# Moving VectorE's squares and state additions one step later, and finding scatter rows one group sooner, in a two-layer kernel

## What is computed

```
x = x + gated_slot_attention(norm(x))   # 16 heads, DK 64, DV 128, 64 slots; two recurrences over time
x = x + fp8_linear(norm(x))
x = x + windowed_attention(norm(x))     # 16 heads of 128, rope, window 64
x = x + routed_experts(norm(x))         # 64 experts, top 4, plus 2 shared experts
```

```
hk = hk * g_t + k_t x p_t ;  ok = q_t . hk          # state S of the kernel
pv = softmax(ok)
hv = hv * g_t + p_t x v_t ;  o = pv . hv            # state R of the kernel
o = o * rsqrt(mean(o*o) + eps) * weight * silu(x Wg) ;  y = o Wo
```

```
top-4 of (logits + bias); scores = softmax(logits) at these, divided by (their sum + 1e-8)
out = sum over the 4 experts of score * expert(x), plus shared experts
```

## Time and profile before

| what | us |
|---|---|
| median of 3 runs | 2103.16 |
| the profiled execution | 2105.88 |
| its span in the trace | 2104.1 |
| PE busy | 1841.9 (88%) |
| PEld busy | 1547.6 (74%) |
| DVE busy | 1371.7 (65%) |
| ACT busy | 847.8 (40%) |
| POOL busy | 828.3 (39%) |

### The profile page before, as it was taken

The page is one execution under the profiler, slowest core; times in us unless marked ns, Lnnn a source line. Parts: engine busy times, 40 slices in busy tenths (PEclk is TensorE's granted clock), DMA queues, the critical chain, the costliest instruction groups (busy, mean ns, idle before and its releaser), DMA issues. The chain is left out here.

```text
span 2104.1 us, 39769 instructions
## 1 busy us (share of the span) xinstructions
PE 1841.9 (88%) x13586; PEld 1547.6 (74%) x13587; DVE 1371.7 (65%) x2986; ACT 847.8 (40%) x2008; POOL 828.3 (39%) x1165
## 2 busy tenths in 40 slices
PE   5999999999999999982699999999999967749990
PEld 3788788887888778871388888888888845647870
DVE  5766676667666677766766766666776647514445
ACT  3434443444433443431355555555555531213330
POOL 3332432333332432334443444444443324636661
PEclk9999999999999999995699999999999957969995
DMA  2100010000950000000110010010000051366655
GB/s 89 46 0 0 0 46 0 0 0 20 357 4 0 1 1 0 0 0 8 63 41 0 1 41 0 0 41 0 0 1 0 0 197 52 103 167 192 191 174 219
DMA packets 72760, 108.20 MB, mean 51 GB/s; under 512 B 24988, under 2 KB 53980, under 8 KB 72028
## 3 DMA queue, kind: packets, MB, share of 16 engines
q1 hardware_dynamic: 62300, 77.38, 12.7%
q0 software_dynamic: 9216, 25.44, 3.3%
q10 hardware_dynamic: 1152, 4.19, 0.5%
HBM read 62.17 MB, written 45.09 MB: 51 GB/s over the span
## 5 line engine op out<-in xcount | busy, mean ns | idle before, releaser
L1394 POOL TENSOR_TENSOR b_rot<-b_by_cos,b_by_sin 128x512 f32<-128x512 f32 x128 | 164.8, 1287 | 363.0 <-DVE b_by_sin L1296 359.3
L791 POOL TENSOR_TENSOR a_ms<-a_ms,a_esq 128x4 f32<-128x4 f32 x64 | 12.7, 199 | 469.4 <-DVE a_ms L691 469.4
L1872 POOL DMA_INDIRECT ys<-m_yb,m_dest x128 | 122.8, 959 | 85.1 <-issue 68.4
L680 DVE TENSOR_TENSOR a_mix_m<-a_ps_av,square_consts 128x512 f32<-128x512 f32 x64 | 44.3, 692 | 121.9 <-PE a_ps_av L432 121.9
L1254 ACT ACTIVATE b_prob<-b_sc,b_nmax 128x128 f32<-128x128 f32 x256 | 99.7, 391 | 52.6 <-DVE b_nmax L1338 52.6
L598 DVE RECIPROCAL a_rz<-a_ps_sz 128x256 f32<-128x256 f32 x64 | 112.5, 1758 | 3.4 <-PE a_ps_sz L344 3.4
L557 ACT ACTIVATE a_sq<-a_ps_og 128x512 f32<-128x512 f32 x64 | 38.2, 597 | 175.8 <-PE a_ps_og L452 160.4
L691 DVE TENSOR_REDUCE a_ms<-a_sq 128x4 f32<-128x512 f32 x64 | 43.9, 685 | 86.8 <-ACT a_sq L557 86.8
L1145 PE MATMUL b_ps_o<-b_pT,b_V 128*128 128x64 f32 x512 | 100.0, 278 | 0.0
L1145 PE MATMUL b_ps_o<-b_pT,b_Vs 128*128 128x64 f32 x512 | 96.6, 271 | 0.7 <-ACT b_pT L1227 0.7
L1308 DVE TENSOR_TENSOR b_oT_lo<-b_ps_o,b_oT_hi 128x512 fp32r<-128x512 f32 x64 | 44.3, 692 | 67.1 <-ACT b_oT_hi L1232 67.1
(11 more groups left out here) (344 smaller groups left out, 6321.6 us busy)
## 6 DMA issues: line engine op xcount, KB each, us to landing
xs<-a_zeros SPq DMA_DIRECT2D x32, 528.0 KB, 14.4
m_xb<-xs SPq DMA_DIRECT2D x32, 528.0 KB, 4.2
wgu_all<-wgu SPq DMA_DIRECT2D x4, 2048.0 KB, 14.3
m_wd<-wd SPq DMA_DIRECT2D x2, 2048.0 KB, 17.5
f_got<-ys SPq DMA_DIRECT2D x8, 512.0 KB, 14.3
f_got<-ys ACTq DMA_DIRECT2D x8, 512.0 KB, 14.3
X<-x SPq DMA_DIRECT2D x2, 1024.0 KB, 7.2
a_w_raw<-Wv SPq DMA_DIRECT2D x4, 512.0 KB, 6.4
```

What stands on the lines that cost most here:

```text
L680: nc.vector.tensor_tensor(pairs(mix_m[:, b, :, :]), ps_as, tri.unsqueeze(1).unsqueeze(1).broadcast_to([P, 2, 2, P]), ALU.mult).then_inc(c[ ...
L1394: nc.gpsimd.tensor_tensor(rot[:, i, :, :], by_cos[:, i, :, :], by_sin[:, i, :, :], ALU.add)\
L1872: pool.indirect_dma_start(ys, bass.IndirectOffsetOnAxis(ap=dest[:, i % RING, j:j + 1], axis=0), yb[:, i % RING, j // 2, j % 2, :], None).t ...
```

## The change

Four edits.

1. Gated-slot stage, VectorE only. The sum of squares and the addition to R of step H leave the end of step H; as `finish(H)` they stand in step H+1, behind its first mask and ahead of `o_norm(H)`. `clip`, which stood ahead of `o_norm`, now stands behind it. The addition to S of step H moves up within its own step, behind `o_low`. The loop is unrolled by one more pair of steps because the first step's `finish` copies where others add.
2. Route and shared stage. The sum of the chosen scores, the reciprocal and the product leave the route stage; in their place four small operations on the picked `gates` (128x64) stand at the end of the shared stage, ahead of the last `sum_up`.
3. Block stage. `find_home(i+1)` stands right behind `x_copy(i+1)`. `dest` has 6 buffers in place of 3, and its wait on `y_sent` is for three groups earlier.
4. Block stage. GpSimd no longer waits for `dest_out`; ScalarE's `y_copy` does.

```diff
             def step(H, b, tile_before, ...):
                 n = 1 - b
                 dve.wait_ge(c["p_at"], done(H))
                 nc.vector.tensor_tensor(pairs(attn_m[:, b, :, :]), ps_as,
...
+                if prev:
+                    finish(H - 1, n, prev_first)
+                    o_norm(H - 1, n)
                 if nxt:
                     clip(H + 1)
-                if prev:
-                    o_norm(H - 1, n)
...
                 if prev:
                     o_low(H - 1, n)
+                dve.wait_ge(c["p_r"], done(H))
+                s_new = ps_s[:, GQ:GQ + 2 * M].rearrange("p (j m) -> p j m", j=2)
+                for a in range(2):
...
+                last.then_inc(c["s_add"], 1)
...
                 if prev:
                     y_add(H - 1, tile_before, final)

-                dve.wait_ge(c["sq_out"], done(H))
-                nc.vector.tensor_reduce(ms[:, b, 0, :], sq[:], AX, ALU.add).then_inc(c["ss_out"], 1)
-
-                dve.wait_ge(c["p_r"], done(H))
...
-                last.then_inc(c["s_add"], 1)
-                dve.wait_ge(c["p_o"], done(H))
...
-                    nc.vector.tensor_tensor(R[:, b, :, :], r_new, R[:, b, :, :], ALU.add).then_inc(c["r_add"], 1)
                 if split_wo is not None and b == 0:
                     wo_high(split_wo)
                 if split_for is not None:
                     low("g", split_for)

+            def finish(H, b, first):
+                dve.wait_ge(c["p_r"], done(H))
+                dve.wait_ge(c["sq_out"], done(H))
+                nc.vector.tensor_reduce(ms[:, b, 0, :], sq[:], AX, ALU.add).then_inc(c["ss_out"], 1)
+
+                dve.wait_ge(c["p_o"], done(H))
...
+                    nc.vector.tensor_tensor(R[:, b, :, :], r_new, R[:, b, :, :], ALU.add).then_inc(c["r_add"], 1)

 # route_stage
-            linked(nc.vector.tensor_reduce(st[:, 2, :], work[:], AX, ALU.add))
-            linked(nc.vector.scalar_tensor_tensor(st[:, 3, :], st[:, 1, :], 1e-8, st[:, 2, :], ALU.mult, ALU.add))
-            linked(nc.vector.reciprocal(st[:, 4, :], st[:, 3, :]))
-            nc.vector.tensor_tensor(comb[:], work[:], over_e(st[:, 4, :]), ALU.mult)
             dve.wait_ge(p_owner, 1)
 # shared_stage
+            dve.wait_ge(gated, NT * TOPK)
+            nc.vector.tensor_reduce(share[:, 0, :], gates[:], AX, ALU.add).then_inc(shared_out, 1)
...
+            nc.vector.tensor_tensor(gates[:], gates[:], share[:, 2, :].unsqueeze(2).broadcast_to([P, NT, TOPK]), ALU.mult)
             sum_up(NTC - 1)
 # block_stage
-        dest = sb("dest", [P, RING, 4], I32)
+        HOMES = 2 * RING
+        dest = sb("dest", [P, HOMES, 4], I32)
...
-                pool.wait_ge(dest_out, i + 1)
...
                 act.wait_ge(p_y, i + 1)
+                act.wait_ge(dest_out, i + 1)
...
-                if i >= RING:
-                    dve.wait_ge(y_sent[i % RING], 64 * (i // RING))
+                if i >= HOMES:
+                    dve.wait_ge(y_sent[i % RING], 64 * (i // RING - 1))
...
                 if i + 1 < NGRP:
                     x_copy(i + 1)
+                    find_home(i + 1)
...
-                find_home(i)
```

More of the change, by code:

```diff
@@ L646, in low, with step @@
                                         ALU.subtract).then_inc(w_low[part], 1)
-            def step(H, b, tile_before, first=False, prev=True, nxt=True, split_wo=None, split_for=None, final=False):
+            def finish(H, b, first):
[3 more added lines that the diff above has]
+                dve.wait_ge(c["p_o"], done(H))
+                r_new = ps_s[:, 0:2 * DV].rearrange("p (j v) -> p j v", j=2)
+                if first:
+                    nc.vector.tensor_copy(R[:, b, :, :], r_new).then_inc(c["r_add"], 1)
+                else:
+                    nc.vector.tensor_tensor(R[:, b, :, :], r_new, R[:, b, :, :], ALU.add).then_inc(c["r_add"], 1)
+            def step(H, b, tile_before, first=False, prev=True, prev_first=False, nxt=True, split_wo=None, split_for=None,
+                     final=False):
                 n = 1 - b
@@ L676, in step @@
                     o_low(H - 1, n)
+                dve.wait_ge(c["p_r"], done(H))
+                s_new = ps_s[:, GQ:GQ + 2 * M].rearrange("p (j m) -> p j m", j=2)
+                for a in range(2):
+                    r = slice(a * DK, (a + 1) * DK)
+                    if first:
+                        last = nc.vector.tensor_copy(S[r, b, :, a, :], s_new[r])
+                    else:
+                        last = nc.vector.tensor_tensor(S[r, b, :, a, :], s_new[r], S[r, b, :, a, :], ALU.add)
+                last.then_inc(c["s_add"], 1)
                 if split_wo is not None and b == 1:
@@ L726, in _ @@
                 final = g == NG - 1
-                step(H0 + 1, 1, 0, first=True, split_wo=g, final=final)
-                with dve.Fori(1, CH - 1) as t:
+                step(H0 + 1, 1, 0, first=True, prev_first=True, split_wo=g, final=final)
+                step(H0 + 2, 0, CH, prev_first=True, final=final)
+                step(H0 + 3, 1, 1, final=final)
+                with dve.Fori(2, CH - 1) as t:
                     step(H0 + t * 2, 0, t + CH - 1, final=final)
@@ L732, in _ @@
                 step(H0 + STEPS - 1, 1, CH - 1, nxt=not final, final=final)
+            finish(NG * STEPS - 1, 1, False)
             o_norm(NG * STEPS - 1, 1)
@@ L1437, with route_stage @@
 HT = D // 2
-def route_stage(nc, xh, xl, ident, tri, ones, xn, s_hi, s_lo, slot, comb, ptop, place, ids, small, raw, wgu, A):
+def route_stage(nc, xh, xl, ident, tri, ones, xn, s_hi, s_lo, slot, comb, ptop, place, ids, total, small, raw, wgu, A):
     with ExitStack() as ctx:
@@ L1468, in route_stage @@
         work = comb
-        st = sb("st", [P, 5, NT])
+        peak = sb("peak", [P, NT])
         chosen = sb("chosen", [P, NT * E_], BF16)
@@ L1696, in scatter_rows, with shared_stage @@
             .then_inc(sent, 16)
-def shared_stage(nc, X, xh, xl, xn, s_hi, s_lo, slot, comb, ptop, place, gates, xs, sent):
+def shared_stage(nc, X, xh, xl, xn, s_hi, s_lo, slot, comb, ptop, place, gates, total, xs, sent):
     with ExitStack() as ctx:
@@ L1712, in shared_stage @@
         picked = sb("picked", [P, 2, E_])
+        share = sb("share", [P, 3, NT])
         ps_g = ctx.enter_context(nc.psum_tensor("e_ps_g", [P, 2, TC], F32))
@@ L1718, in shared_stage @@
             sem(n) for n in ("p_g", "p_u", "p_down", "th_out", "hg_out", "h_out", "hi", "lo", "y_add"))
-        gated = sem("gated")
+        gated, shared_out = sem("gated"), sem("shared_out")
         block = ctx.enter_context(nc.Block())
@@ L2001, in find_home @@
                 dve.wait_ge(order_out, i + 1)
-                if i >= RING:
-                    dve.wait_ge(y_sent[i % RING], 64 * (i // RING))
-                nc.vector.tensor_tensor(dest[:, i % RING, :], order[:, s, :], xb[:, i % RING, :, D + TOPK], ALU.add)\
+                if i >= HOMES:
+                    dve.wait_ge(y_sent[i % RING], 64 * (i // RING - 1))
+                nc.vector.tensor_tensor(dest[:, i % HOMES, :], order[:, s, :], xb[:, i % RING, :, D + TOPK], ALU.add)\
                     .then_inc(dest_out, 1)
@@ L2024, in _ @@
             x_copy(0)
+            find_home(0)
             gated(0)
@@ L2165, in program @@
                 norm_stage(nc, "n2", X, stats, ident, xh, xl, preload=(preload_route, 16 * 15), keep=xn)
-                route_stage(nc, xh, xl, ident, tri, ones, xn, s_hi, s_lo, slot, comb, ptop, place, ids, small, raw, wgu,
-                            A)
-                shared_stage(nc, X, xh, xl, xn, s_hi, s_lo, slot, comb, ptop, place, gates, xs, sent)
+                route_stage(nc, xh, xl, ident, tri, ones, xn, s_hi, s_lo, slot, comb, ptop, place, ids, total, small, raw,
+                            wgu, A)
+                shared_stage(nc, X, xh, xl, xn, s_hi, s_lo, slot, comb, ptop, place, gates, total, xs, sent)
             block_stage(nc, ident, wgu, xn, place, ids, own, sent, xs, ys, A)
```

26 lines of the change are left out of this document (11 added, 15 removed).

## The result

The changed kernel takes 2112.29 us (median of 9 runs, 2110.1 to 2115.4); the kernel before took 2104.77 beside it (9 runs, 2101.39 to 2108.1). The ratio is 1.0036, 95% interval 1.0026 to 1.0047: 7.6 us slower. The profiled execution's span went from 2104.1 to 2112.3. The prediction was 2114.8 (2100 to 2126), slower with 0.78.

What follows compares the result with a forecast made beforehand. It took the gated-slot return path from L384 over VectorE and ScalarE to w as deciding. Terms +10.4, 0, +9.0, -2.3, -5.5 gave +11.6 on 2105.88, 2117.5; less 2.7 for the median, 2114.8 us (2100 to 2126).

Steps and rivals of the forecast that it cites:

- Usual step: Gated-slot stage: late clip lengthens the interval between loads of w by 0.20 us in 52 steps, +10.4 us.
- The faster rival: Gated-slot stage: the wait for the mask is the real stall, so TensorE becomes the limit; 2085 us, chance 0.07.
- Contention: Gated-slot stage: GpSimd's work beside w stretches it by 0.46 per us of overlap, 0.20 when covered in full.
- Change of group: Gated-slot stage, three times: later o_norm and GpSimd split of v delay TensorE's v projection by 3.0 us, +9.0 us.
- much slower: Rival: both gated-slot stretches at upper bound and a lower clock at each change of group; 2129.6 us, chance 0.10.
- Edit 2: Route and shared stage: ids starts sooner, -2.3 us; four small operations fit into 1.78 us of VectorE's wait.
- Block stage: Edits 3 and 4: sooner requests remove TensorE's waits for row loads beyond the first, -5.5 us (-4.1 to -8).
- the lower row: Block stage: the matmuls' idle time without the first wait for row loads, 4.1 us.
- The upper row: Block stage: the weight loads' idle time without the first wait for row loads, 11.2 us.

Runs made afterwards that it cites:

- experiment 4: Kernel 3 with GpSimd's low part of the running sum started only after w is out: 0.9935 of the kernel before, 11.8 us less than kernel 3.
- kernel 3: The changed kernel with clip put back ahead of o_norm, behind finish: 0.9991 of the kernel before, 9.5 us less than the changed kernel.
- experiment 5: The changed kernel with low("g") moved into the group's last step, ahead of o_norm: 0.9964 of the kernel before, 15.2 us less than the changed kernel.
- both repairs: The changed kernel with clip ahead of o_norm and low("g") in the last step behind clip: 0.9944 of the kernel before, median 2093.1 us.
- experiment 12: The kernel before with edits 3 and 4, but find_home's last operation at the old place: 0.9973 of the kernel before, 8.2 us slower than edits 3 and 4.

## Why the prediction was right, and where its terms were off

By its own sum: +10.4 + 0 + 9.0 - 2.3 - 5.5 = +11.6; the trace has +22.6 for the gated-slot stage, -2.3 for edit 2, -11.6 for the block stage and -0.3 for the stretches between, +8.4 to the last scatter and +8.2 at the end. The direction and the time were right; the parts were off in opposite ways, the gated-slot stage by +3.2 (22.6 for 19.4) and the block stage by -6.1 (-11.6 for -5.5), so that the nearness of the sum is in part luck.

*Usual step.* Each link came as forecast: from the load, `o_high` 12.47 (12.46 forecast), L538 12.94 (12.95), L542 13.24 (13.31), w 13.69 (13.76) and 0.59 long (0.63). The next load is at 14.33 in place of 14.44. The mean before, over the 44 steps inside the groups, was 14.22 and not 14.235, as the first group's steps were shorter; against it this is 0.11 in place of 0.20 each, some 5 us in place of 10.4. The 0.11 between 14.33 and 14.44 is 0.06 for L542, which starts 0.30 behind L538, the lower of the two values that I had where I took the middle, 0.04 for w's length, and rounding along the chain. The faster rival (the mask as the real stall) would have needed the exponential before its place; the mask's 18.5 us did vanish and bought nothing by itself.

*Contention.* That GpSimd's work stretches w was right, and experiment 4 shows it. The price was too small: from 0.55 I took 0.46 per us of overlap, yet in kernel 3 w grows by 0.33 while L784 overlaps it for 0.48. A price per us was the wrong form too: 0.12 for 0.26, 0.33 for 0.48 and 0.84 for 0.99 (the split of v beside L645, 3.20 where 2.36 is its time alone) are each the overlap less some 0.15. The last section has more on this. That w would be covered in full by `e_low` and both chunk copies was wrong too: in the changed kernel `e_low` is itself stretched, and only the copies reach w.

*Change of group: the term that failed, in size.* The mechanism was right: the split of v starts 3.61 later from the load (3.68 forecast) and the projection 2.65 later (3.0 taken). What I left out is the other side. In the step ahead of it ScalarE's copy of w_hi (1.03 us) stands between the late exponentials and `o_high`, so that step takes 15.42 for 14.13; and the projection ran at the lower clock at all three changes, behind a gap of 2.7 us on TensorE each time, which I had kept for the rival "much slower". At the first change the three steps around it cost 1.3, 4.2 and 0.65, together 6.1; the second cost 3.5, as it had been slow before as well (17.03), and the third 5.5. That is 15.1 in place of 9.0. Experiment 3 took away the first part; experiment 5 most of the second, and with both repairs the clock stayed at 1.00 at all three changes. The rest of the 22.6, some 2.6 us, lies at the stage's end: its last two steps take 14.68 and 14.69 for 14.13 and 14.09, and from the last load of w to the last `o_norm` are 10.89 us (965.61 to 976.50) where they were 9.43 (944.47 to 953.90); the granted clock of that stretch was below full speed before as well, 0.83, and is about 0.65 now.

*Edit 2* gave its 2.3. The four small operations lie in VectorE's wait, which is 0.89 now and was 1.78.

*Block stage: the second term off in size.* It was priced by the waits for rows beyond the first, 4.1 to 11.2, and set near the lower row because the matmuls' wait seemed the harder evidence. The turns say 0.34 x 30 = 10.2 and 1.5 more at the tail. The upper row, the idle time of the weight loads, was the right one. The loop shows it without any wait row: 6.26 from a group's transposes to the next gated product, `find_home`'s 0.6 and the load's 4.2 make 11.06 for two turns, or 5.53 a turn, where the turns took 5.55. That fit was found with the result in hand, and experiment 12, which forecast by it, measured 5.36 for 5.43. With the request 2.25 behind the transposes and three turns to go round, the loop no longer binds.

## What to carry to other kernels

When an instruction is moved ahead of a short one that another engine waits for, follow the short one's engine to the end of its chain: here clip came 1.5 us later, and the usual step grew by 0.11 us although the mask's wait of 0.39 was gone. Look at what the other engine runs beside the instruction that ends the critical loop; one wait that pushed it behind brought 9 us in the old order and 12 in the new one. And price a stall inside a loop by the loop's length, transfer included, not by the waits that one engine shows.

## What was not expected of the hardware

Which of two overlapping operations is stretched depended on which came first. VectorE's subtraction started 0.02 ahead of GpSimd's L766 (408.75 and 408.77): VectorE's kept 0.43 and GpSimd's took 1.01 in place of 0.73. GpSimd's L784 started 0.27 ahead of w: it kept 0.75, and w took 0.76 in place of 0.43. In both pairs the later one was longer by about as much as the earlier one still had to run, less some 0.15. So was w in the kernel before, 0.55 with 0.26 of L775 left and 0.63 with 0.35 left (401.24), and GpSimd's split of v, 2.78 in kernel 5 with 0.57 of L645 left. Over the traces of the kernel before, the changed one and kernels 3 and 5, from 100 to 900 us, there are 524 pairs of such operations (GpSimd's beside one of VectorE with both inputs in SBUF) in which the earlier one had 0.2 us or more left; in all of them the later one was longer by what was left less 0.09 to 0.17. An operation with an input from PSUM was not touched: VectorE's L608 in the changed kernel starts at 410.66, two hundredths behind GpSimd's L783 (410.64), and takes its 0.67, and L783 its 0.73. No run here varied sizes or order for its own sake, so this holds for the operations of this stage; why some 0.15 is spared isn't shown.

The Trainium skill (GPSIMD Engine Reference, section Specifications) has the contention for VectorE instructions with two SBUF inputs. The pairs and L608 agree with it. It also says (Perfetto Trace Analysis, section GPSIMD Engine Instruction) to time GpSimd by the distance of starts and not by the reported length. By that L766 still takes longer: its successor starts 0.96 behind it in the changed kernel (409.73), and 0.67 behind it in kernel 3, where VectorE's subtraction comes 1.2 us later.
